# Layer-1 attention as one run of slots: normalisation in two small products, maxima in one transfer

## The reference, cut to what matters

```python
# x: (8, 256, 128); H = 16 heads of 8; 8 chunks of 256 tokens, causal inside a chunk
h = layernorm(x) * (1 + ca) + sa
q, k, v = split_heads(h @ Wq.T), split_heads(h @ Wk.T), split_heads(h @ Wv.T)
scores = einsum('bhnqd,bhnkd->bhnqk', q, k) / sqrt(8)
scores = where(causal, scores, -inf)
attn = softmax(scores, axis=-1)
out = einsum('bhnqk,bhnkd->bhnqd', attn, v)
x = x + ga * (out @ Wo.T)
h = layernorm(x) * (1 + cb) + sb      # then the router: top 2 of 8 experts
```

## Time and profile before

| | us |
|---|---|
| median of 3 executions | 724.79 (723.13 to 727.91) |
| profiled execution, its own time | 723.68 |
| its span, first to last instruction | 721.9 |
| between its span and its time | 1.8 |
| mean granted TensorE clock | 0.853 of full speed |
| layer-1 attention, first front to last logits | 317 to 540 |

### The profile page before, as it was taken

The page is one execution under the profiler, slowest core; times in us unless marked ns, Lnnn a source line. Parts: engine busy times, 40 slices in busy tenths (PEclk is TensorE's granted clock), DMA queues, the critical chain, the costliest instruction groups (busy, mean ns, idle before and its releaser), DMA issues.

```text
span 721.9 us, 12550 instructions
## 1 busy us (share of the span) xinstructions
PE 509.8 (71%) x4141; PEld 394.5 (55%) x4141; DVE 384.3 (53%) x985; ACT 261.9 (36%) x694; POOL 325.8 (45%) x414
## 2 busy tenths in 40 slices
PE   6689999932776787712789789968732788878870
PEld 5456566521765677611656456544321688878860
DVE  4678888449344443444777554544229334343335
ACT  1322232010444344312136444535400555555532
POOL 3623443221566666554124444536621455565633
PEclk9899999655699989965689898989855699999995
DMA  6313222220111111116563443532320111111116
GB/s 201 99 47 104 63 63 73 61 59 0 34 44 42 42 42 41 41 51 160 140 144 93 122 119 81 131 56 47 67 66 2 27 41 38 37 42 37 41 35 170
DMA packets 57808, 50.59 MB, mean 70 GB/s; under 512 B 8896, under 2 KB 50368, under 8 KB 56960
## 3 DMA queue, kind: packets, MB, share of 16 engines
q1 hardware_dynamic: 40272, 28.51, 15.8%
q10 hardware_dynamic: 12480, 11.04, 5.2%
q0 software_dynamic: 4992, 10.23, 5.2%
HBM read 36.85 MB, written 12.91 MB: 69 GB/s over the span
## 4 chain that ended last, share of the span: by engine, by line
PE 41%; DVE 14%; DMA 12%; issue 11%; SPq 6%; POOL 4%; another core or an unknown queue 4%; ACT 4%; DVEq 1%; ACTq 1%; POOLq 0%
PE bank L782 11%; PE pair L793 6%; DMA max_d<-qk 4%; PE pair L782 3%; PE pair L609 3%; PE bank L624 3%; DVE xh L947 2%; PE bank L860 2%; PE pair L846 2%; PE bank L580 2%; PE bank L769 2%; SPq L440 2%; PE pair L826 1%; SPq L422 1%
## 5 line engine op out<-in xcount | busy, mean ns | idle before, releaser
L782 PE MATMUL bank<-probs,stack_q 128*128 128x128 f32 x708 | 102.8, 294 | 39.5 <-ACT probs L1419 27.0
L1636 POOL DMA_INDIRECT ye_d<-probs,dst_row x78 | 79.9, 1025 | 89.5 <-DVE probs L1197 39.4
L782 PEld LDWEIGHTS bank<-probs,stack_q 128*128 128x128 f32 x708 | 91.4, 203 | 47.9 <-ACT probs L1419 32.9
L1630 POOL DMA_INDIRECT probs<-h_d,src_row x78 | 76.0, 974 | 38.3 <-issue 19.2
L793 PE MATMUL pair<-qk,stack_k 128*128 128x128 f32 x624 | 87.8, 286 | 2.5 <-DVE stack_k L1205 1.6
L793 PEld LDWEIGHTS pair<-qk,stack_k 128*128 128x128 f32 x624 | 79.8, 200 | 4.9 <-issue 4.5
L1684 POOL TENSOR_SCALAR_AFFINE_SELECT probs<-probs 128x256 f32<-128x256 f32 (+1 forms) x96 | 46.4, 487 | 75.9 <-ACT probs L1509 75.5
L1509 ACT ACTIVATE probs<-pair 128x512 f32<-128x512 f32 x96 | 56.7, 598 | 48.4 <-PE pair L846 47.8
L1184 DVE COPY qk<-W 128x512 f32 x78 | 34.1, 438 | 44.7 <-issue 24.9
L860 PE MATMUL bank<-probs,V 128*32 128x256 f32 (+1 forms) x512 | 52.5, 339 | 4.1 <-POOL probs L1684 3.9
L826 PE MATMUL pair<-stack_k,stack_q 96*128 96x128 bf16 (+1 forms) x256 | 42.1, 276 | 18.8 <-DMA stack_k<-parts_d 12.1
(11 more groups left out here) (193 smaller groups left out, 995.3 us busy)
## 6 DMA issues: line engine op xcount, KB each, us to landing
W<-in_w ACTq DMA_DIRECT2D x16, 256.0 KB, 4.0
mod_bc<-mod_d SPq DMA_DIRECT2D x16, 192.0 KB, 5.7
parts_d<-parts SPq DMA_DIRECT2D x8, 384.0 KB, 3.5
W_up<-in_up_w ACTq DMA_DIRECT2D x8, 256.0 KB, 4.3
h_d<-h_tok SPq DMA_DIRECT2D x16, 128.0 KB, 2.1
rot<-ye_d SPq DMA_DIRECT2D x16, 128.0 KB, 2.7
W<-in_gate_w ACTq DMA_DIRECT2D x8, 256.0 KB, 3.2
W<-in_down_w ACTq DMA_DIRECT2D x8, 256.0 KB, 4.0
```

The source lines that it names most:

```text
L782: i = pe.matmul(at[r % 2][:, k * P:(k + 1) * P], w_now[:, r % 2, which, k * P:(k + 1) * P], x_t[:, r % 2, :], start=True, stop=True)
L1630: gp.indirect_dma_start(out=x_rows[:, n % RING, :], out_offset=None, in_=h_d[l], in_offset=bass.IndirectOffsetOnAxis(ap=src_row[:, n:n + 1 ...
L1636: gp.indirect_dma_start(out=ye_d[l], out_offset=bass.IndirectOffsetOnAxis(ap=dst_row[:, n:n + 1], axis=0), in_=y_rows[:, n % RING, :], in_ ...
```

## The change

- Slots: `group_at(s, g, lead)` counts slots over all steps, so maxima and exponentials of consecutive batches follow each other without a break. Maxima of batch b run from slot 4 of step b+1 to slot 3 of step b+2 (`MAX_LEAD` = 16), exponentials in step b+3, back in b+4, logits in b+5. Steps are -1 to 12, two fewer.
- Maxima in one transfer: `max_t` (32 rows: head, part) goes from SBUF to rows 48 to 79 of `stack_q`, repeated for all 16 heads; `stack_k` holds in those rows a one where row and head match. This pattern is made once by one GpSimd instruction in layer 0 and copied by four transfers (`spread_heads`) before step 0. The memsets of `set_stack` go.
- Outputs stay on chip: every score group is four cells of 128 by 128, 16 heads go to one bank (Y0 or P2 by turns), 16 rows per head, of which 8 are outputs and one the denominator. `dens_by_token` (four float32 products with 8 columns each), a reciprocal on VectorE, a widening copy on ScalarE, `spread_dens` (four float32 products with 128 columns) and a multiplication on VectorE (`divide`) take the place of `unpad_y`, `load_y` and `spread_den`. `project_out` has two products per output tile in place of one, as rows are half filled.
- Only the 8 groups on the diagonal are masked by GpSimd. The mask of the maxima is one product per group in place of two or four.
- SyncE's order: pair, mod, `store_parts(s)`, `stack_max(s-2)`, `load_stacks(s)`, `store_h(s-4)`. The stacks of batch s are now loaded in step s.
- Values are copied in two pieces; their buffers are set by 8 GpSimd memsets (and one for `den_wide`) before step -1, in place of one.

```diff
-LAG = {0: ..., 1: dict(scores=2, max_rows=3, probs=4, dens=5, back=6, route=7, last=7)}
+LAG = {0: ..., 1: dict(max_rows=2, mods=3, back=4, logits=5, last=5)}
+def group_at(s, g, lead):
+    k = SLOTS * s + g - lead
+    return divmod(k, SLOTS) if 0 <= k < NB * SLOTS else (None, None)
+EXP_LEAD = SLOTS * LAG[1]["mods"]
+MAX_LEAD = SLOTS + MAX_LATE                     # 12 + 4
 def exp_cells(g):
+    s0, t0 = ((0, 0), (0, P), (P, P))[g % 3]
+    return [(4 * (g // 3) + n, s0, t0, P) for n in range(4)]
 def stack_max(b):
     sp.wait_ge(sem["max_t"], b + 1)
-    sp.dma_start(max_d[b % 2], max_t[0:2 * H, b % 2, :])
-    sp.wait_ge(sem[f"max_out{b % 2}"], 16 * (b // 2 + 1))
-    sp.dma_start(stack_q[MAX_ROW:MAX_ROW + 2, b % STACKS, :], max_d[b % 2]...)
+    sp.dma_start(stack_q[MAX_ROW:STACK_ROWS, b % STACKS, :].rearrange("p (h t) -> p h t", h=H),
+                 max_t[0:2 * H, b % 2, :].unsqueeze(1).broadcast_to((2 * H, H, T)))
+def spread_heads():
+    for r in range(STACKS):
+        sp.dma_start(stack_k[MAX_ROW:STACK_ROWS, r, :], stack_k[P - 2 * H:P, 0, :])
@@ SyncE, steps of layer 1
-    load_stacks(1, s - 1); load_y(1, s - 5); stack_max(s - 3); store_parts(1, s)
-    spread_den(s - 5); store_h(1, s - 7); unpad_y(1, s - 4)
+    store_parts(1, s); stack_max(s - 2); load_stacks(1, s); store_h(1, s - 4)
@@ TensorE
-    for n, at in enumerate(diag_blocks):
-        i = pe.matmul(ps[:, at:at + P], ident_b[:, :], neg_mask[:, :], ...)
+    pe.matmul(blocks, ident_b[:, :], neg_mask[:, :].unsqueeze(1).broadcast_to((P, len(cells), P)), ...)
+def dens_by_token(b):
+    pe.wait_ge(sem["softmax_y"], b + 1)
+    for k in range(4):
+        i = pe.matmul(P1[:, 8 * k:8 * k + 8], y_keep[:, b % 2, k * P:(k + 1) * P], const("den_rows"), ...)
+def spread_dens(b):
+    pe.wait_ge(sem["den_wide"], b + 2)
+    for k in range(4):
+        i = pe.matmul(P1[:, k * P:(k + 1) * P], den_wide[:, k]..., const("ident"), ...)
 for g in range(SLOTS):
+    exp_scores(at lead EXP_LEAD - 1); max_scores(at lead MAX_LEAD - 1); softmax_pv(at lead EXP_LEAD + 1)
+    g == 0: transpose_x(s), route_logits(s-5)   g == 2: project_qk(s), dens_by_token(s-4)
+    g == 4: spread_dens(s-4)    g == 6: project_out(s-4), max_to_rows(s-2)
+    g == 8: project_v(s)        g == 11: transpose_h2(s-4)
@@ VectorE
+    g == 2: rest_of_qk(s)   g == 3: invert_dens(s-4)   g == 5: divide(s-4)
@@ ScalarE
+    g == 1: y_keep <- bank   g == 3: den_wide <- den_inv   g == 6: max_t <- bank   g == 8: keep_v(s)
@@ GpSimd
-def set_stack(r): two memsets, steps 0 and 1 of both layers
+gp.tensor_scalar(stack_k[:, 0, :] (16 x 256), iota broadcast, const("stack_head"), None, ALU.is_equal)
-gp.memset(V[:, :, :, :], 1.0)
+8 memsets of v_packed, one of den_wide
```

More of the change, by code:

```diff
@@ L530, in _ @@
                     load_pair(0, s + 2)
[L531 to L536, removed]
+                if s == -1:
+                    spread_heads()
+                if b["mods"] is not None:
+                    load_mod(1, b["mods"])
+                if b["front"] is not None:
+                    store_parts(1, b["front"])
                 if b["max_rows"] is not None:
@@ L539, in _ @@
                 if b["front"] is not None:
[L540 to L546, removed]
+                    load_stacks(1, b["front"])
+                if b["back"] is not None:
+                    store_h(1, b["back"])
             load_gb(1)
@@ L875, in _ @@
-                if w is not None:
-                    exp_scores(w, 0)
-                if m is not None:
-                    max_scores(m, 0)
-                for g in range(13):
-                    if w is not None and g + 1 < 12:
-                        exp_scores(w, g + 1)
-                    if m is not None and g + 1 < 12:
-                        max_scores(m, g + 1)
-                    if w is not None and g >= 1:
-                        softmax_pv(w, g - 1)
+                a, mx, z, y = b["front"], b["max_rows"], b["back"], b["logits"]
@@ L893, in _ @@
                         project_qk(1, a)
-                    if g == 7 and y is not None:
+                    if g == 2 and z is not None:
+                        at_least(pe, sem["v_1"], cnt(s - 1), base["v_1"])
+                        at_least(pe, sem["logits1"], cnt(s - 5), base["logits1"])
+                        dens_by_token(z)
+                    if g == 4 and z is not None:
+                        spread_dens(z)
+                    if g == 6 and z is not None:
+                        project_out(1, z)
@@ L1674, in _ @@
                     mix3(0, 1)
[L1675 to L1682 removed]
+                for g in range(SLOTS):
+                    w, i = group_at(s, g, EXP_LEAD)
+                    if w is not None and is_diagonal(i):
+                        gp.wait_ge(sem["exped"], SLOTS * w + i + 1)
+                        cells = probs[:, i % 4, :].rearrange("p (n t) -> p n t", t=P)
```

349 lines of the change are left out of this document (181 added, 168 removed).

## The result

| | before | changed |
|---|---|---|
| median of 4 executions, us | 723.96 (722.41 to 727.91) | 745.13 (732.70 to 754.98) |
| ratio to before | | 1.0152, 95% interval 1.0085 to 1.0218 |
| profiled execution, span | 721.9 | 730.9 |
| mean granted TensorE clock | 0.853 | 0.833 |
| first parts stored to last logits of layer 1 | 328.48 to 540.41, 211.9 us | 321.52 to 549.72, 228.2 us |

The forecast was 705 us (694 to 718). The interval lies above 1, so the change made the kernel slower, by 1 to 2%.

A forecast was written before the change was run, and what follows sets the result against it. Bound: SyncE's queue order in mid-attention (21.5 to 22 us per step), the DRAM round trip at its end. Layer 1 -18.0 and layer 0 -1.0 give span 702.9, profiled 704.7; median 1.1 above, forecast 705 us (694 to 718).

The forecast's parts named there:

- a full step afterwards, by TensorE: Layer-1 attention: step 5's 16.9 us, less PV savings, plus new products, gives 19.1 us per step (18.0 to 20.5).
- rival 2: Full attention steps: no stalls, TensorE's clock stays at full speed, 18 us per step, 698 us in all; chance 0.18.
- The signs that it named: New trace, layer-1 attention: slot 3 of step 4 at 389, last PV at about 508, last logits 14 us behind.
- 478 + 15.4 + 13.7: Layer-1 attention: end of step 8 at 478, step 9 takes 15.4 us, step 10 13.7, ending at 507.7.
- The queue and the loop by transfers, 18 us: SyncE's queue loses its waits except on parts; parts 3.5, stack loads 10.5, way back 4: 18 us per step.
- The new transfer of the maxima: SBUF to SBUF, 256 KB, issued near slot 7, needed at slot 11: hidden at 3.5 to 4.5 us.
- Rival 3: Maxima's transfer lands 9 us or more after issue, TensorE stands at slot 11 every step: slower, 732 us; chance 0.05.
- rival 1: Transfers bind all full steps: 714 to 720 us; chance 0.18 shared with rival 4 (710 to 717), 0.09 for 717 to 732.
- Rival 4: Queue's release shows nothing, TensorE's work fills 22 us anyway; only start and tail count: 712 us; 0.18 shared with rival 1.
- The tail: Step 11, end of layer-1 attention: 14.7 us from end of step 10 to last logits, at 522.4 for 540.4.
- The start of layer 1, -3.7: Step 0 of layer-1 attention: set_stack's memsets no longer stretch a norm_apply, so everything there starts 3.7 us earlier.
- Layer 0, pattern 3.6 us long, +2: Layer 0: one-hot pattern takes 3.6 us at the memset's rate, costing +2 against -3.0 for memsets, -1.0 net.

The follow-up runs named there:

- full rows: Changed kernel with maxima over 96 rows and exponentials over 128, set_stack's memsets back: 709.1 us, 0.989 of before.
- one with the same two changes per slot whose clock had risen at 375: Changed kernel with 128-row stacks, pattern in pieces, maxima over 48 of 96 rows: 717.6 us, 1.007 of before; again 719.0 us, 0.995.
- the pattern in pieces: Changed kernel with the one-hot pattern written in 16 GpSimd pieces over steps 2 to 9 of layer 0: 735.5 us, 1.017 of before; again 738.0, 1.017.
- the other two such kernels: Changed kernel with full rows and pattern in pieces: 672.3 us, 0.987 of before; the same with maxima ahead of exponentials: 705.2 us, 0.986.
- best version: Changed kernel with 128-row stacks (maxima over 96 rows) and the one-hot pattern in 16 pieces: 672.3 us, 0.987 of before.
- the side-by-side run with 80 rows: Changed kernel with pattern in pieces (maxima 48 rows, exponentials 80), run again beside the 128-row-stack kernel on one chip: 738.0 us, 1.017 of before.
- experiment 5: Changed kernel with each slot's maxima and mask put ahead of the exponentials: median 720.3 us, no ratio; with full rows and pieces 705.2 us, 0.986.
- experiment 6: Changed kernel with 128-row stacks and pattern in pieces: 0.987 of before; with maxima over 48 rows 1.007, again 0.995, beside 80-row exponentials at 1.017.

## Why the prediction was wrong, point by point

- **The step that failed: "a full step afterwards, by TensorE", 19.1 us.** Its prices were read from products of 96 and 128 rows and carried to products of 48 and 80. The missing term is two changes per slot, 12 x 0.2 = 2.4 us of TensorE's work per step. At full clock the step measured 20.5 to 20.7 us, 1.5 over the forecast, and with full rows 19.2 to 19.6, at 18.5 to 18.9 of TensorE: as a price list for the old shapes the sum was right. Over the whole attention the changes come to 6 to 10 us (207.7 against 197.5 to 202.0, above), well under the 96 x 0.2 = 19 us of added work.
- **The clock: the larger part, and a term put at nothing.** The sum took full clock for every full step, and rival 2 argued that without stalls it would stay up. It was 0.50 from 334 to 405 us with TensorE never idle from 360 on, and fell again near 485 and 520. The steps from the fourth to the sixth store of parts (373.98 to 403.86 to 427.98) took 29.9 and 24.1 us; with full rows they took 18.7 and 19.3. These two steps alone are 16 of the 228.2 - 197.5 = 30.7 us by which attention is longer, and 228.2 - 207.7 = 20.5 us separate the changed kernel from one with the same two changes per slot whose clock had risen at 375. In the table the six kernels with short maxima have mean clocks of 0.811 to 0.852, the seven with tall ones 0.845 to 0.873; among the executions in the ratios the changed kernel (with the pattern in one or in pieces) has 0.809 to 0.834, the one with full stacks and maxima over 48 rows 0.837 to 0.865. That the changed kernel's short products go with a lower clock is shown, what lowers the clock is not.
- **The signs that it named.** Slot 3 of step 4 came at 398.6 us for 389, the last products with V at 533.2 for 508, the last logits at 549.7 for 522.4.
- **Two slips in its sum.** 478 + 15.4 + 13.7 is 507.1, not 507.7, and 704.7 + 1.1 is 705.8, not 705. Neither changes the outcome.
- **The queue and the loop by transfers, 18 us: right as far as it can be seen.** The first stack loads landed 9.6 us after the first issue (324.77 to 334.41) for 10.5 taken. With full rows TensorE waited 1.0 us in all for stacks between 380 and 508, so the steps go by TensorE; the 18 us themselves were never the bound there and are not measured.
- **The new transfer of the maxima: right.** 3.1 us against 3.5 to 4.5 taken, hidden. Rival 3, the only one on the slower side, needed 9 us and was the wrong mechanism; rival 1 did not come. Rival 4 had the right engine as the bound, for another reason and at 712 us.
- **The whole of attention.** From first parts stored to last logits the forecast had 522.4 - 324.8 = 197.6 us. With full rows it is 197.5, and 201.5 and 202.0 in the other two such kernels. That the first meets it to 0.1 us is luck in part: it had some 31 us of half clock ahead of the full steps, which the forecast had no term for.
- **The tail: 14.7 us from the end of step 10, that is 14.1 from the last copy of a bank; measured 15.8** (533.89 to 549.72), 15.5 with full rows, at half clock most of the way.
- **The start of layer 1, -3.7: nearly right.** First parts stored 7.0 us earlier, of which 4.0 were there before routing 0 (before had a stretch of half clock at 130 us that the changed kernel had not); 2.9 remain.
- **Layer 0, pattern 3.6 us long, +2: the size was wrong.** The instruction took 10.6 us: a memset's rate does not hold for a compare that reads float32 and writes bf16. The normalised rows of batch 0 came 7.3 us later (copied at 19.83 for 12.57), but the steps behind took part of that up: with the pattern in pieces routing 0 began 4.1 us earlier in the changed kernel (150.91 for 154.99) and 2.0 us earlier with full rows (158.96 for 160.97), and neither time moved beyond its interval.
- **Where the rest of the gain went.** Forecast 0.973, best version 0.987. Full rows need the memsets back, so the 3.7 us of the start and the 1.0 of layer 0 are not to be had; 14.3 of the 19.0 us are left, 0.980, at the lower end of its interval. Where the remaining 0.7% lies is not shown.

## What to carry to other kernels

Before two products are put beside each other, look at their mode (contraction above or up to 64 rows, outputs 128 or 32 wide): each change cost 0.1 us here, as much as some 230 columns at full clock (512 took 0.22), and rows padded with zeros, from 72 up to 128, cost TensorE nothing (only the memsets that write them). So a layout that saves rows, memory or transfers can cost time on an engine whose products take as long with 72 rows as with 128. Waits that the added work can fill take back part of it (2.4 us became 1.3 per step here). And when TensorE is made the bound, price its work from rows of the new shape, and give the clock a range of its own.

## What was not expected of the hardware

- 0.1 us at each change between a product of up to 64 rows and one of 72 or more, at half clock as at full (0.54 against 0.42 for 512 columns).
- TensorE busy by the trace without a gap for 40 us at half clock (360 to 400 us), while the kernel with full rows reached full clock by 380 and kept it to 508. In the profiled execution of the side-by-side run with 80 rows (763.85 us) half clock lasted from before 360 to 469, again without a gap:

```profile
400.00:440.00 40.00, 40.00 (x267) 22.02 (x267) 17.07 (x41) 11.15 (x24) 11.67 (x17) 0.50 0.29 75
```

- With short maxima, going from the stack of 128 rows to that of 80 cost 1 to 2% of the time. Whether few rows or drained changes hold the clock down stays open: taking away one change per slot (experiment 5) and taking 128 rows for the exponentials (experiment 6) both brought full clock at 375 or 376 us in the profiled executions.
- A GpSimd compare of 4096 elements per partition, float32 in, bf16 out, took 10.6 us, and a VectorE operation with two SBUF inputs beside it took 6.6 us in place of 0.19; it ended 1.7 us before the compare did.
